# Mamba, mixture of experts and linear attention on one core: the last two groups' scatters with eight transfers under way instead of four

## The reference, cut to what matters

```python
logits = x_flat @ gate_w.T
scores = jax.nn.softmax(logits, axis=-1)
_, topk_ids = jax.lax.top_k(scores, 2)          # 2 of 8 experts for each token
w = scores * one_hot(topk_ids).sum(axis=1)
g, u = split(x_flat @ experts_gate_up[e].T)      # 176 + 176 columns
expert_out[:, e] = (silu(g) * u) @ experts_down[e].T
out = sum_e w[:, e] * expert_out[:, e] + sigmoid(x_flat @ shared_expert_gate_w.T) * shared
x = x + 0.5 * out
```

## Time and profile before

| | |
|---|---|
| time, median of 3 runs | 906.46 us (906.28 to 907.28) |
| the profiled execution's own time | 916.95 us |
| its span | 915.6 us |
| TensorE busy | 838.3 us (92%), mean granted clock 0.966 |
| VectorE busy | 633.4 us (69%) |
| ScalarE busy | 514.6 us (56%) |
| GpSimd busy | 503.2 us (55%), 589 instructions |

### The profile page before, as it was taken

How to read it: one execution, slowest core, us unless ns; L and a number is a source line. 1 busy time by engine, 2 the same in 40 slices (tenths; PEclk the granted TensorE clock), 3 DMA queues, 4 the chain that set the end, 5 groups by cost and what they waited for, 6 DMA issues and landing times.

```text
span 915.6 us, 16102 instructions
## 1 busy us (share of the span) xinstructions
PE 838.3 (92%) x4924; PEld 637.2 (70%) x4924; DVE 633.4 (69%) x2152; ACT 514.6 (56%) x1047; POOL 503.2 (55%) x589
## 2 busy tenths in 40 slices
PE   7999899999999999999989999989899998989981
PEld 7668586758578587676767677856777776577761
DVE  5397678896766866888568956779665568834452
ACT  3877657757877558367655535634564455314430
POOL 3169363768344388764654456268333627667553
PEclk8999899999999999899999999999999999989996
DMA  9600000001011012111122123111122321122332
GB/s 296 273 1 1 0 1 1 2 18 39 14 37 35 27 38 64 41 47 36 50 84 73 42 89 99 30 41 46 53 84 89 108 60 47 59 76 85 91 120 95
DMA packets 66245, 57.10 MB, mean 62 GB/s; under 512 B 7739, under 2 KB 59195, under 8 KB 65947
## 3 DMA queue, kind: packets, MB, share of 16 engines
q1 hardware_dynamic: 57235, 37.65, 13.5%
q0 software_dynamic: 8640, 17.74, 6.3%
q10 hardware_dynamic: 288, 0.67, 0.3%
HBM read 27.39 MB, written 28.65 MB: 61 GB/s over the span
## 4 chain that ended last, share of the span: by engine, by line
PE 43%; POOL 19%; issue 13%; DVE 12%; DMA 8%; ACT 5%; SPq 0%; POOLq 0%; DVEq 0%; ACTq 0%
PE psum L803 9%; PE psum L534 8%; PE psum L823 6%; POOL sorted_x L1752 5%; POOL c_y L1780 4%; POOL sent_y L1795 2%; POOL sorted_l L1752 2%; PE psum L614 2%; DMA sorted_x<-g_xn,r_slot 1%; PE psum L529 1%; DMA sent_y<-e_y,l_to 1%; PE psum L738 1%; DMA e_sx<-sorted_x 1%; PE psum L743 1%; PE psum L573 1%
## 5 line engine op out<-in xcount | busy, mean ns | idle before, releaser
L1752 POOL DMA_INDIRECT sorted_x<-g_xn,r_slot x96 | 96.1, 1001 | 83.0 <-DVE r_slot L1237 47.0
L1780 POOL DMA_INDIRECT c_y<-sorted_y,r_slot x96 | 93.4, 973 | 69.3 <-DMA sorted_y<-e_y 31.8
L803 PE MATMUL psum<-gu_w,e_sx 128*128 x368 | 127.7, 477 | 1.2 <-ACT e_sx L1409 0.7
L823 PEld LDWEIGHTS psum<-d_w,e_h 88*128 88x128 f32 x736 | 91.2, 193 | 14.8 <-issue 11.7
L823 PE MATMUL psum<-d_w,e_h 88*128 x736 | 99.1, 279 | 2.3 <-ACT e_h L1409 1.5
L1258 DVE TENSOR_TENSOR e_h<-e_h,psum 128x352 f32<-128x352 f32 x96 | 47.8, 502 | 64.6 <-ACT e_h L1588 64.4
L803 PEld LDWEIGHTS psum<-gu_w,e_sx 128*128 128x128 f32 x368 | 66.8, 197 | 34.9 <-issue 14.9
L1588 ACT ACTIVATE e_h<-psum 128x352 f32<-128x352 f32 x96 | 42.9, 451 | 83.4 <-PE psum L803 83.0
L1409 ACT ACTIVATE e_h<-psum 88x512 f32<-88x512 f32 x96 | 54.6, 573 | 52.2 <-PE psum L534 51.3
L529 PE MATMUL psum<-ones 128*128 128x128 f32 x520 | 73.0, 283 | 3.5 <-POOL ones L1819 1.9
L529 PEld LDWEIGHTS psum<-ones 128*128 128x128 f32 x520 | 67.2, 199 | 8.9 <-issue 3.4
(11 more groups left out here) (246 smaller groups left out, 2069.7 us busy)
## 6 DMA issues: line engine op xcount, KB each, us to landing
e_sx<-sorted_x SPq DMA_DIRECT2D x66, 128.0 KB, 2.2
sorted_y<-e_y SPq DMA_DIRECT2D x66, 128.0 KB, 1.8
m_cv<-sorted_l SPq DMA_DIRECT2D x22, 130.0 KB, 2.3
xs<-in_x SPq DMA_DIRECT2D x8, 256.0 KB, 6.7
sorted_x<-c_y SPq DMA_DIRECT2D x4, 512.0 KB, 14.0
sorted_l<-c_y SPq DMA_DIRECT2D x4, 512.0 KB, 16.9
c_y<-sent_y SPq DMA_DIRECT2D x8, 256.0 KB, 3.6
out<-xs SPq DMA_DIRECT2D x7, 256.0 KB, 2.5
```

The lines of the kernel that those rows point to most:

```text
L803: last = e.matmul(two.banks[j].tile[:, 0:2 * IEXP], e_xT[k % 4][:, j * P:(j + 1) * P], gu_w[:, bass.ds(which[j] * (2 * IEXP), 2 * IEXP)], ...
L823: last = e.matmul(bank.tile[:, j * P:(j + 1) * P], e_hT[s][0:IHALF, (2 * j + c) * P:(2 * j + c + 1) * P], d_w[:, bass.ds(which[j] * (2 * D ...
L1752: e.indirect_dma_start(out=sorted_x[n] if g < LAST else sorted_l[g - LAST], out_offset=bass.IndirectOffsetOnAxis(ap=r_slot[n][:, k, t:t + ...
L1780: e.indirect_dma_start(out=c_y[i % 2][:, k, j, :], out_offset=None, in_=sorted_y[n], in_offset=bass.IndirectOffsetOnAxis(ap=r_slot[n][:, k ...
```

## The change

The scalars of the plan (CHUNK_AT, FINISH_AT, SORTED_AT and so on) become lists with the same number for every block or group. For groups 6 and 7 the scatters count on two semaphores in turn: the first and third four of a group on scatter0 or scatter1 as before, the second and fourth on a new one, slid, that both groups share. Before a four GpSimd waits for what its own semaphore counts, that is for the four before the last four. SyncE's loads wait for both semaphores. Everything else is written as before and planned anew.

```diff
+            def moved_to(g, begun):
+                if g < LAST:
+                    return f"scatter{g % 2}", moved_by(g // 2 * TOPK * NT, begun)
+                four = begun // UNDER_WAY
+                if four % 2:
+                    return "slid", 16 * (TOPK * NT // 2 * (g - LAST) + four // 2 * UNDER_WAY)
+                return f"scatter{g % 2}", 16 * (g // 2 * TOPK * NT + four // 2 * UNDER_WAY)
+
...
-                        moved = moved_by(g // 2 * TOPK * NT, TOPK * t)
+                        moved = moved_to(g, TOPK * t)
                         yield (T + 8.0 + 2.0 * t, 2.5, ("r_slot", g + 1), zeros, ("g_xn", i + 1),
-                               ("sx0", loaded[0]), ("sx1", loaded[1]), ("sx2", loaded[2]), ("sx3", loaded[3]),
-                               (f"scatter{n}", moved))
+                               ("sx0", loaded[0]), ("sx1", loaded[1]), ("sx2", loaded[2]), ("sx3", loaded[3]), moved)
...
-                        on.wait_ge(f"scatter{n}", moved)
+                        on.wait_ge(*moved)
                         for k in range(TOPK):
...
-                                in_=g_xn[i % KEPT][:, j, :] if g < LAST else l_xn[i - GB * LAST][:, j, :], in_offset=None).then_inc(*S.up(f"scatter{n}", 16, ROWS))
+                                in_=g_xn[i % KEPT][:, j, :] if g < LAST else l_xn[i - GB * LAST][:, j, :], in_offset=None
+                            ).then_inc(*S.up(moved[0], 16, ROWS))
...
                 if g >= LAST:
-                    yield T, 0.0, (f"scatter{n}", 16 * 16 * (g // 2 + 1)), ("e_gu", k - 3), ("sent_to", k - 3 - LAST * PAIRS)
-                    on.wait_ge(f"scatter{n}", 16 * 16 * (g // 2 + 1))
+                    here, slid = 16 * TOPK * NT * (g // 2) + 8 * TOPK * NT, 8 * TOPK * NT * (g - LAST + 1)
+                    yield (T, 0.0, (f"scatter{n}", here), ("slid", slid), ("e_gu", k - 3), ("sent_to", k - 3 - LAST * PAIRS))
+                    on.wait_ge(f"scatter{n}", here)
+                    on.wait_ge("slid", slid)
```

More of the change, by code:

```diff
@@ L83 @@
 ATANH = [2.0 / (2 * k + 1) for k in range(8)]
-STEP = 25.1
-MAMBA_AT = 16.3
-CHUNK_AT = 29.3
+FIRST = [0.0, 25.1, 50.2, 75.3, 100.4, 125.5, 150.6, 175.7]
+MAMBA = [16.3, 41.4, 66.5, 91.6, 116.7, 141.8, 166.9, 192.0]
+CHUNK_AT = [29.3, 29.3, 29.3, 29.3, 29.3, 29.3, 29.3, 29.3]
 GAP = 4.91
@@ L92 @@
 FOLD_AT = 37.6
[L93 to L97, removed]
+FINISH_AT = [12.7, 12.7, 12.7, 12.7, 12.7, 12.7, 12.7, 12.7]
+AGAIN = [3.26, 3.26, 3.26, 3.26, 3.26, 3.26, 3.26, 3.26]
+GATED_AT = [25.2, 25.2, 25.2, 25.2, 25.2, 25.2, 25.2, 25.2]
+SORTED_AT = [7.0, 7.0, 7.0, 7.0, 7.0, 7.0, 7.0, 7.0]
+PAIR_AT = [23.9, 23.9, 23.9, 23.9, 23.9, 23.9, 23.9, 23.9]
 PACE = 3.12
-COMBINED_AT = 19.3
-KV_AT = 145.8
+COMBINED_AT = [19.3, 19.3, 19.3, 19.3, 19.3, 19.3, 19.3, 19.3]
@@ L101 @@
+KV_AT = [145.8, 145.8, 145.8, 145.8, 145.8, 145.8, 145.8, 145.8]
 SECOND_AT = [161.0, 194.0, 193.0, 266.0, 411.0, 456.0, 575.0, 545.0]
-GATED_AGAIN_AT = 47.0
-FIRST = [STEP * b for b in range(NBLK)]
-MAMBA = [t + MAMBA_AT for t in FIRST]
+GATED_AGAIN_AT = [47.0, 47.0, 47.0, 47.0, 47.0, 47.0, 47.0, 47.0]
 TAPPED_BY = [sum(len(TAPPED[k // BLK_PER_BATCH]) for k in range(b)) for b in range(NBLK + 1)]
 FOLDED_BY = [XBC_CHUNKS * b - n for b, n in enumerate(TAPPED_BY)]
-CHUNK = [[t + CHUNK_AT + GAP * j for j in T4] for t in MAMBA]
@@ L109 @@
[L109 to L115, removed]
@@ L116 @@
-KV = [COMBINED[b] + KV_AT for b in range(4)] + [max(COMBINED[b] + KV_AT, SECOND[b - 4] + 16.0) for b in range(4, NBLK)]
+CHUNK = [[t + at + GAP * j for j in T4] for t, at in zip(MAMBA, CHUNK_AT)]
+FINISH = [t[3] + at for t, at in zip(CHUNK, FINISH_AT)]
+FFN0 = sorted([(FIRST[b], 0, b) for b in range(NBLK)] + [(FINISH[b] + AGAIN[b], 1, b) for b in range(NBLK)])
+SECOND = [175.7 + t for t in SECOND_AT]
+GATED = [t + at for t, at in zip(FINISH + SECOND, GATED_AT + GATED_AGAIN_AT)]
+SORTED = [GATED[GB * g + GB - 1] + SORTED_AT[g] for g in range(ROUNDS * NGROUP)]
@@ L117 @@
+PAIR = [[SORTED[g] + PAIR_AT[g] + PACE * k for k in range(PAIRS)] for g in range(ROUNDS * NGROUP)]
+COMBINED = [PAIR[i // GB][-1] + COMBINED_AT[i // GB] + 10.0 * (i % GB) for i in range(ROUNDS * NBLK)]
+KV = [COMBINED[b] + KV_AT[b] for b in range(4)] + [max(COMBINED[b] + KV_AT[b], SECOND[b - 4] + 16.0) for b in range(4, NBLK)]
 FFN0_AT = {(again, b): i for i, (_, again, b) in enumerate(FFN0)}
@@ L125 @@
 g_var g_rstd g_shift g_xn g_turn g_xT g_logits g_sub g_sgexp g_exp g_any g_weight s_gate s_up s_silu s_h s_down s_res
-r_before r_rank r_free r_slot r_expert zero0 zero1 scatter0 scatter1
+r_before r_rank r_free r_slot r_expert zero0 zero1 scatter0 scatter1 slid
 sx0 sx1 sx2 sx3 e_tr e_xT e_gu e_silu e_h e_trh e_hT e_down e_y sy0 sy1 sy2 sy3 sent_to sent0 sent1 added gather0 gather1 c_add store
```

## The result

The changed kernel takes 905.27 us, the median of 20 runs (900.01 to 910.14), where the kernel before takes 909.86 in 20 runs beside them (903.38 to 914.78). The ratio, estimated from all these runs, is 0.9945 (the two medians alone give 0.9950), with a 95% interval from 0.9926 to 0.9965: 5.0 us less, between 3.2 and 6.7. From the 906.46 of the forecast that is 901.5. The profiled execution after has a span of 908.1 us and a time of 909.48, so both profiled executions are slower than their medians. I therefore compare distances from the first scatter of group 6, not absolute times.

What follows compares the result with a forecast made beforehand. GpSimd's scatters, landings and sends were taken to set the pace from 782 us on. Of 8.08 us of waits removed, 2 find no e_y; the lead sums to 6.2 us: 906.46 - 6.2 = 900.3, range 897.0 to 905.0.

Steps and rivals of the forecast that it cites:

- step 4: Start of group 6's experts: sorted rows usable by TensorE at 806.4 instead of 812.25, gates' work over just in time.
- step 6: First send to end: lead holds at 6.0 to 6.8 us, nothing swallows it; sum 6.2 us, last send at +115.8.
- (1): Plan constants as lists: they hold what the scalars did, to the rounding of a sum; no rank changes.
- (2): GpSimd's four waits on transfers just issued: 3.18 us in group 6 and 4.90 in group 7 go, 0 left.
- (3): Two group 7 scatters leave group 6's middle; group 6's last scatter starts at 801.15 instead of 806.93: 5.78 us.
- (5): First send of group 6 starts at 817.1 to 817.7 instead of 823.28: 5.6 to 6.2 us earlier.
- the 2 of the forecast: At the first sends: the other 2 us of the 8.08 removed find no e_y to send.
- (7): Scatters beside busy VectorE: a skill rule implies stretching, 13 us if all 16 took 1.793; the 0.97 us says none.
- B: Rival: only group 6's own waits count, group 7's pair staying or TensorE's gates holding the start; 3.2 us, 903.3; chance 0.11.
- C: Rival: more gain, all 8.1 us of waits or the clock's 1.8 us on top; 898.4, up to 10; chance 0.08.
- D: Rival: no gain, lead lost at the combine, in longer landings or dearer scatters; 906.5; chance 0.11.
- E: Rival: slower, group 6's combine slides forward among TensorE's pairs; three pairs make it 3.3 us slower, 909.8; chance 0.08.

Runs made afterwards that it cites:

- the kernel before with pauses: Kernel before plus two pauses in the 602 to 632 us row; its profile is the other one of the old order: 911.22 us, ratio 1.0020.
- held condition: State of the first two experiment sets, where the kernel before took 934.05 and 934.00 us instead of 909.85; named for what it does to TensorE.
- changed kernel run again: The changed kernel, unaltered, timed again against the kernel before: 950.64 us, ratio 1.0176, where the kernel before took about 934 us.
- the residual first: Changed kernel with VectorE's residual of the gates of blocks 14 and 15 put before its slot-to-place operations: 952.03 us, ratio 1.0194 to the kernel before.
- the old waits: Changed kernel's order of every engine, but one count per group, so the old waits return: 933.46 us, ratio 1.0000 to the kernel before.

## Why the prediction was right, step by step

The forecast was 900.3 us, a gain of 6.2. Measured are 5.0 (3.2 to 6.7), or 901.5. The mechanism is the one forecast up to the first send. Two places were wrong: the start of the experts (step 4) and the combine, which takes in part of the lead (step 6).

**(1) The constants.** No effect, as said (1.0019, interval across 1). "No rank changes" was a little too strong: one stage in group 1 changes places.

**(2) The four waits.** All gone, and what is left of the new ones is nothing beyond the 0.30 us of any step, as taken.

**(3) The order.** Group 6's last scatter was to start 19.12 us behind the first and starts at 19.24. Group 7's pair has left the middle.

**(4) The start of the experts.** Here a term was mis-sized. The transposes were forecast 24.37 us behind the first scatter (806.4 less 782.03) and came at 26.72. Of the 2.35 us, 0.2 are the scatters and their landing, 0.48 the load (3.43 in the chain instead of 2.95), and 1.67 the wait for a bank. I had looked for what would be late next on TensorE alone, and found its gates' work over in time. It was; but that work hands its bank back through an instruction of VectorE, which the planner now places behind one that waits for the load itself. In the kernel before, the residuals stood in front of it. About 1.1 us came back at once, since the clock's dip was shorter: the eight matmuls of L801 took 3.23 us instead of 4.34, and the granted clock over the 7 us around the first transposes and these matmuls (from 806) was 0.76, where it was 0.53 over the like 7 us before. This is the row:

```profile
806.00:813.00 7.00, 4.81 (x16) 3.28 (x16) 4.13 (x19) 2.00 (x5) 5.38 (x6) 0.76 0.25 79
```

(Window, length, busy time of TensorE, its weight loads, VectorE, ScalarE and GpSimd, then clock, DMA share, GB/s.)

**(5) The first send.** Forecast 35.1 to 35.7 us behind the first scatter, seen 36.18: a lead of 5.07 instead of 5.6 to 6.2. It waits 0.70 us for e_y, so the late start of step 4 shows here, softened by the shorter dip.

**(6) To the end.** The last send was forecast at +115.8 and came at +115.96. That looks better than it is. Against the other profile of the same order (+119.13) the lead is 3.2 us, against the one shown (+121.95) it is 6.0. The step from first to last send differs by 2.7 us between two profiles of one order, so a single pair of profiles doesn't prove the last microseconds. The runs do, with 5.0. GpSimd's waits from 778 to 905 us (who waited for whom: us in all, times, longest), in the kernel before and then after:

```profile
POOL sent_y L1795 <- DMA sent_y<-e_y,l_to: 10.0, 4, 3.1
POOL sorted_l L1752 <- DMA sorted_l<-m_cv,r_slot: 9.3, 4, 2.8
...
POOL sent_y L1795 <- DVE e_y L1262: 4.0, 1, 4.0
POOL sent_y L1795 <- DVE l_to L1282: 3.3, 2, 3.0
```

```profile
POOL sent_y L1803 <- DMA sent_y<-e_y,l_to: 13.2, 6, 3.1
...
POOL sent_y L1803 <- DVE e_y L1260: 7.9, 5, 6.3
```

To compare them, take from each wait the 0.3 us of any step. The four waits of 9.3 us are the ones removed: 8.1. In front of sends there were 17.3 us in seven waits, that is 15.2, and 0.45 of a step of 0.75 us without a reason: 15.6. In the kernel after there are 21.4 us in twelve: 17.8. So 2.2 of the 8.1 came back, near the 2 of the forecast, and 5.9 are left, the lead of 6.0 seen. The other profile of the old order had 7.8 us to remove and 13.0 in front of sends (14.8 in six waits); against it 4.8 came back and 3.0 are left. The 5.0 of the runs lie between the two.

One place takes in lead against either profile: the 28th send, the second block of group 7. The lead falls there from 8.2 to 5.1 us against the profile shown, from 4.8 to 2.4 against the other. GpSimd waits there for the block before to land in all three profiles (in the kernel after until 865.69). But in the changed kernel e_y is late as well: its last matmuls end at 862.0, and VectorE copies it only at 867.69, behind group 6's combine:

```profile
862.41 1.26 DVE L1298 SCALAR_TENSOR_TENSOR xs<-c_y,r_score,xs 128x128 f32<-128x128 f32 x4 [0.20 <-DMA c_y<-sent_y]
...
864.16 3.61 DVE L1298 SCALAR_TENSOR_TENSOR xs<-c_y,r_score,xs 128x128 f32<-128x128 f32 x12 [0.49 <-DMA c_y<-sent_y]
867.69 0.42 DVE L1260 COPY e_y<-psum 128x256 f32<-128x256 f32 x1
```

In the old order this copy stood in front of the combine. In the kernel before it is at 868.06 and the combine at 870.73; in the kernel before with pauses:

```profile
862.57 0.42 DVE L1263 COPY e_y<-psum 128x256 f32<-128x256 f32 x1
864.97 4.91 DVE L1301 SCALAR_TENSOR_TENSOR xs<-c_y,r_score,xs 128x128 f32<-128x128 f32 x16 [1.97 <-DMA c_y<-sent_y]
```

So the sentence of the forecast that nothing there can swallow the lead was wrong: by these profiles the new order costs 2.4 to 3.1 us at this send. No run with the copy put back in front of the combine was made, so what that would bring at the end stays open. That the last send came within 0.2 us of the forecast is in part luck: against the profile shown the lead had grown to 8.2 us, beyond the forecast's 6.8, and fell again here.

**(7) The rule against the change.** The scatters that moved beside a busy VectorE took what they took before:

```profile
L1759 POOL DMA_INDIRECT sorted_l<-m_cv,r_slot x32: 965/969/1063, 780.5 to 830.7; - x32
```

By the Trainium skill (DMA: Bandwidth & Descriptors, "SWDGE vs HWDGE vs iDMA") they might have stretched where VectorE is in a fast mode. The median of 0.969 us, with VectorE busy 21.44 of the 25 us from 775 to 800, shows none of it here. Whether any of VectorE's instructions there ran in such a mode the trace doesn't say, so the rule itself isn't tested.

**The rivals.** B (3.2 us, only group 6's waits) lies at the edge of the interval; its reason, that TensorE holds the start, was half right: a bank held it, for 1.67 us. C and D are excluded by the interval. Of E the beginning is seen and it has a price. Group 6's combine starts 81.9 us behind the first scatter instead of 88.7, or of 86.2 in the other profile of the old order. In VectorE's order it slid forward past one copy of e_y, not by the two or three pairs from which E would have decided, and that goes with the 2.4 to 3.1 us of step 6.

What I had in no case is a condition of the machine in which the same change costs 1.8%.

## What to carry to other kernels

A drain on the path is worth its length less what comes back further down the same queue: list, for the queue that is sped up, its next waits, and expect them to take a part (here 3.1 of 8.1 us by the runs). A new order can also move work of another engine in front of what the queue needs: look for the one instruction that changed places with the longest one. When a load is brought forward, ask of the engine that uses it not only whether it is free but who empties the buffer it writes, and where that instruction stands in its own queue (1.67 us here). A wait that seems pure loss may also be the only pause in a row of transfers issued by GpSimd, so time such a change under more than one set of conditions before it is kept.

## What the runs showed of the hardware

Shown: the kernel before ran at 909.86 and 909.85 us in two sets and at 934.05 and 934.00 in two others, one chip appearing among both kinds. In the held condition TensorE has many pauses without a wait (0.3 to 2.5 us each in the changed kernel run again, once 5.1 and once 11.0 in two others) while GpSimd issues indirect transfers without a pause. The ordinary profiles have three in rows of eight and more from 560 us on, of 0.7 to 1.0 us, each between two groups of transposes. TensorE's signals reach VectorE and ScalarE late, by 17 us in the stall shown, mostly 0.1 to 3.0 us after a row of 12 to 20 has ended; twice one came within such a row (809.99 with the residual first, 824.62 with group 7's new waits alone). The ordinary profiles have no wait for "remote" of over 0.8 us. The six kernels that there have rows of 12 to 20 in groups 6 and 7 ran 0.95 to 1.94% above the kernel before. The two with rows of at most eight, the lists alone and the changed kernel with GpSimd's waits of 1.6 to 2.3 us every fourth transfer, ran level with it, though VectorE waits for "remote" there too, 2.9 to 6.1 us at a time from 780 us on. In the changed kernel run again the earliest pauses come 9.4 us into a row (791.4 in the one from 782.0), in the row from 602.3 at 616.5; with group 7's new waits alone one comes 5.7 us into a row (794.5 in the one from 788.8). So no length that is safe can be read from these. The transfers themselves don't take longer there: a scatter takes 0.97 us and the steps are 1.27 us in both conditions.

Not shown: what the condition is, and by what path GpSimd's issuing holds TensorE. The pauses made to test whether breaking the rows alone cures the stall ran when the condition was gone, so that the cure is a pause rather than a count is argued from the old waits only.
